# Routing stage of a graph and mixture-of-experts kernel: another way to the gate logits, and the sums formed on VectorE

## The reference

```python
# layer 1: messages along 25000 edges, sorted by their target row
H = layernorm(x).astype(f16);  v = edge_weight.astype(f16)
x = x + segment_sum(H[dst] * v[:, None], src)        # row to gather: dst, row to add to: src
# layer 2: a mixture of 8 experts, each token goes to one
h = layernorm(x)
logits = h @ gate_w + gate_b                          # (50000, 8)
probs = softmax(logits);  idx = argmax(probs);  prb = probs[idx]
pos = running count of idx, in token order            # place in the expert's queue
kept = pos < C                                        # C = ceil(1.25 * 50000 / 8)
y = relu(buf[e] @ w1[e] + b1[e]) @ w2[e] + b2[e]      # per expert, on its queue
x = x + nan_to_num(y * prb * kept)
```

## Time and profile before

| | us |
|---|---|
| median of three runs | 3391.64 |
| the profiled execution | 3385.78 |
| its span | 3384.2 |
| routing stage: first `slot_i` to last `slot_i` (48 steps) | 703.26 to 1252.62 |
| busy in the span: PE, DVE, ACT, POOL | 2856.8, 2205.4, 1627.8, 1881.3 |

### The profile page before, as it was taken

How to read it: one execution, slowest core, us unless ns; L and a number is a source line. 1 busy time by engine, 2 the same in 40 slices (tenths; PEclk the granted TensorE clock), 3 DMA queues, 4 the chain that set the end, 5 groups by cost and what they waited for, 6 DMA issues and landing times.

```text
span 3384.2 us, 63776 instructions
## 1 busy us (share of the span) xinstructions
PE 2856.8 (84%) x20366; PEld 2577.6 (76%) x20367; DVE 2205.4 (65%) x5550; ACT 1627.8 (48%) x2915; POOL 1881.3 (56%) x1680
## 2 busy tenths in 40 slices
PE   5733323289899976999999999999999999999998
PEld 4733223278788866989889898989899889898987
DVE  7934343377766644677766767777767676767766
ACT  3412121156655644555554555555555555555554
POOL 7788888756766765436354334536343454335333
PEclk8766666678867868999999999999999999999999
DMA  9644443386766623112112111212111121111111
GB/s 375 193 77 71 69 88 58 52 321 230 245 207 221 234 75 101 45 39 74 39 50 69 44 45 45 67 36 71 45 50 44 42 69 48 44 43 47 41 46 45
DMA packets 182245, 322.06 MB, mean 95 GB/s; under 512 B 97649, under 2 KB 124348, under 8 KB 166256
## 3 DMA queue, kind: packets, MB, share of 16 engines
q0 software_dynamic: 89696, 146.98, 16.7%
q1 hardware_dynamic: 92288, 172.66, 15.0%
q10 hardware_dynamic: 144, 1.05, 0.1%
HBM read 186.52 MB, written 138.79 MB: 96 GB/s over the span
## 4 chain that ended last, share of the span: by engine, by line
PE 57%; DVE 3%; issue 1%; DVEq 0%; POOL 0%; DMA 0%; SPq 0%; ACT 0%; POOLq 0%
PE u_Y L1353 29%; PE u_H L1339 26%; PE u_T L1321 2%; DVE y L1283 1%; DVE y L1278 1%; DVE yo L1297 1%; DVE yo L1294 0%; DVE low L1288 0%; DVE yo L1292 0%; DVE hlo L1265 0%; POOL u_x L1141 0%; DVEq L1264 0%; DMA u_x<-out_x,u_rec 0%; DVE u_token L1291 0%; DMA u_rec<-slots 0%
## 5 line engine op out<-in xcount | busy, mean ns | idle before, releaser
L1166 POOL DMA_INDIRECT out_x<-yo,u_token x348 | 435.8, 1252 | 761.0 <-DVE yo L1299 664.2
L1353 PE MATMUL u_Y<-whi,hhi 128*128 128x256 f32 x2784 | 788.2, 283 | 22.2 <-DVE hlo L1265 22.2
L1216 ACT ACTIVATE hm<-u_H,b1e 128x512 f32<-128x512 f32 (+1 forms) x736 | 489.0, 664 | 644.5 <-PE u_H L1339 618.9
L1353 PE MATMUL u_Y<-wlo,hhi 128*128 128x256 f32 x2784 | 779.7, 280 | 0.0
L1353 PE MATMUL u_Y<-whi,hlo 128*128 128x256 f32 x2784 | 779.4, 280 | 0.0
L1141 POOL DMA_INDIRECT u_x<-out_x,u_rec x380 | 396.5, 1043 | 363.4 <-issue 330.0
L1339 PE MATMUL u_H<-xhi,whi 128*128 128x512 f32 (+1 forms) x1472 | 571.5, 388 | 10.1 <-issue 10.1
L1339 PE MATMUL u_H<-xlo,whi 128*128 128x512 f32 (+1 forms) x1472 | 564.8, 384 | 0.0
L1339 PE MATMUL u_H<-xhi,wlo 128*128 128x512 f32 (+1 forms) x1472 | 564.5, 384 | 0.0
L1353 PEld LDWEIGHTS u_Y<-whi,hhi 128*128 128x128 f32 x2784 | 526.1, 189 | 25.3 <-DVE hlo L1265 25.3
L1353 PEld LDWEIGHTS u_Y<-wlo,hhi 128*128 128x128 f32 x2784 | 526.1, 189 | 0.0
(11 more groups left out here) (154 smaller groups left out, 4710.5 us busy)
## 6 DMA issues: line engine op xcount, KB each, us to landing
x<-in_x SPq DMA_DIRECT2D x49, 1024.0 KB
out_x<-x SPq DMA_DIRECT2D x49, 1024.0 KB, 5.0
agg<-zeros SPq DMA_DIRECT2D x25, 1024.0 KB
at<-agg SPq DMA_DIRECT2D x49, 512.0 KB, 5.8
raw<-in_L_ffn_w POOLq DMA_DIRECT2D x14, 1024.0 KB
src_row<-in_src SPq DMA_DIRECT2D x25, 512.0 KB, 4.8
slots<-rec,slot_i POOLq DMA_INDIRECT x392
u_x<-out_x,u_rec POOLq DMA_INDIRECT x380
```

Source lines behind the costliest of these rows:

```text
L1166: pool.indirect_dma_start(out=out[:, :], out_offset=bass.IndirectOffsetOnAxis(ap=token[:, s:s + 1], axis=0), in_=yo[:, s, :], in_offset=No ...
L1216: act.activation(hm[:, f, cols], ps_H[:, f % 2, cols], ACT.Relu, bias=b1e[:, f:f + 1])\
L1353: last = pe.matmul(ps_Y[:, s, 0:D], a[:, f, rows], w2_at(w, buf, f), start=(f == 0 and j == 0), stop=(f == KF - 1 and j == 2))
```

## The change

`aggregate`, its PSUM tile and the f16 identity go: VectorE adds the sums straight from `at` in SBUF. SyncE's load of `at` now waits for that addition. The four banks that this frees go to the turned rows, which now have four banks, and to the logits across (`ps_G`, 8 partitions by 1024 tokens).

`gate` now holds the gate weights (8 columns) and streams 256 turned tokens per product. ScalarE adds the bias as it copies `ps_G` to `across` (`add_bias`, two instructions of 8 by 512). `turn_back` transposes `across` back in eight small pieces, so that the tokens lie on partitions again and VectorE's `choice` reads the same `logits` tile as before. The bias product and `fill` go. The order on TensorE and ScalarE is written anew.

```diff
@@ SyncE, load @@
-                    sp.wait_ge(agg_up, s + 1 - AGGS)
+                    sp.wait_ge(x1_ready, s + 1 - AGGS)
@@ ScalarE @@
+            def add_bias(i, r):
+                s = RING * i + r
+                if not (isinstance(i, int) and s < 1):
+                    act.wait_ge(logits_ready, s)
+                for half in range(2):
+                    act.wait_ge(gated, BANKS * s + 2 * half + 2)
+                    part = slice(half * (STEP // 2), (half + 1) * (STEP // 2))
+                    act.activation(across[:, part], ps_G[:, part], ACT.Identity, bias=gb[:, 0:1])\
+                        .then_inc(across_ready, 1)
...
                 normalise(0)
                 normalise(1)
+                if not (isinstance(i, int) and s < 1):
+                    add_bias(*before_of(i, r, 1))
                 if not (isinstance(i, int) and s == LAST):
                     deviation(*next_of(i, r))
-                copy(0)
                 normalise(2)
-                copy(1)
                 normalise(3)
-                copy(2)
-                copy(3)
+                for k in range(BANKS):
+                    copy(k)
@@ TensorE @@
-            def aggregate(i, r):
...
-                for g in range(k * G // BANKS, (k + 1) * G // BANKS):
-                    for kd in range(KD):
-                        last = pe.matmul(logits[:, g, :], hT[:, g * KD + kd, :], gw[:, kd, :],
-                                         start=False, stop=(kd == KD - 1), skip_group_check=True)
-                if k == BANKS - 1:
-                    last.then_inc(gated, 1)
...
+                if not (isinstance(i, int) and s < 1) and k % 2 == 0:
+                    pe.wait_ge(across_ready, 2 * (s - 1) + k // 2 + 1)
+                part = hT[:, k * PER_BANK:(k + 1) * PER_BANK, :].rearrange("p (g kd) c -> p kd g c", kd=KD)
+                wide = STEP // BANKS
+                for kd in range(KD):
+                    last = pe.matmul(ps_G[:, k * wide:(k + 1) * wide], gw[:, kd, :], part[:, kd],
+                                     start=(kd == 0), stop=(kd == KD - 1))
+                last.then_inc(gated, 1)
+
+            def turn_back(i, r):
+                s = RING * i + r
+                pe.wait_ge(across_ready, 2 * (s + 1))
+                if not (isinstance(i, int) and s < 1):
+                    pe.wait_ge(hot_ready, s)
+                pe.nop(nofuse=True)
+                for g in range(G):
+                    last = pe.transpose(logits[:, g, :], across[:, g * P:(g + 1) * P], ident[0:E, 0:E])
+                last.then_inc(logits_ready, 1)
...
                 turn(i, r, 0)
                 turn(i, r, 1)
-                if isinstance(i, int) and s == 0:
-                    aggregate(0, 2)
-                else:
-                    rank(*before_of(i, r, 1))
-                    fill()
-                gate(i, r, 0)
-                turn(i, r, 2)
-                gate(i, r, 1)
-                turn(i, r, 3)
-                if not (isinstance(i, int) and s == 0):
-                    fill()
-                gate(i, r, 2)
-                if not (isinstance(i, int) and s > LAST - 3):
-                    aggregate(*((i, r + 3) if r + 3 < RING else (i + 1, r + 3 - RING)))
+                if not first:
+                    turn_back(*before_of(i, r, 1))
+                turn(i, r, 2)
+                turn(i, r, 3)
+                gate(i, r, 0)
+                gate(i, r, 1)
+                gate(i, r, 2)
+                if not first:
+                    rank(*before_of(i, r, 1))
                 gate(i, r, 3)
@@ VectorE @@
-                v.wait_ge(agg_up, s + 1)
+                v.wait_ge(agg_loaded[r % AGGS], 16 * ((RING // AGGS) * i + r // AGGS + 1))
                 v.wait_ge(x_loaded[r], 16 * (i + 1))
-                v.tensor_tensor(x1[:, r], ps_A[:], x1[:, r], ALU.add).then_inc(x1_ready, 1)
+                v.tensor_tensor(x1[:, r], at[:, r % AGGS], x1[:, r], ALU.add).then_inc(x1_ready, 1)
...
-                v.wait_ge(gated, s + 1)
+                v.wait_ge(logits_ready, s + 1)
```

More of the change, by code:

```diff
@@ L429, in route_tokens @@
     b1r = sb("b1r", [B1, P], F32)
-    gb = sb("gb", [P, E], F32)
-    ident16 = sb("ident16", [P, P], F16)
+    gb = sb("gb", [E, 1], F32)
+    across = sb("across", [E, STEP], F32)
     stats = sb("t_stats", [P, G, 6], F32)
@@ L454, in route_tokens @@
     ones, before, ident, eps = t["ones"], t["before"], t["ident"], t["eps"]
[L456 to L457 removed]
+    ps_T = ctx.enter_context(nc.psum_tensor("ps_T", [P, 4, 4, P], F32))
+    ps_G = ctx.enter_context(nc.psum_tensor("ps_G", [E, STEP], F32))
     ps_L = ctx.enter_context(nc.psum_tensor("ps_L", [P, 512], F32))
@@ L499, in route_tokens @@
     gated = sem("gated")
+    across_ready = sem("across_ready")
+    logits_ready = sem("logits_ready")
     hot_ready = sem("hot_ready")
@@ L510, in route_tokens @@
     BANKS = G * KD * P // 512
+    assert BANKS == 4
     PER_BANK = G * KD // BANKS
@@ L647, in copy @@
                 def copy(k):
-                    if k == 0 and not (isinstance(i, int) and s < 1):
-                        act.wait_ge(gated, s)
+                    if not (isinstance(i, int) and s < 1):
+                        act.wait_ge(gated, BANKS * (s - 1) + k + 1)
                     act.wait_ge(turned, BANKS * s + k + 1)
                     part = slice(k * PER_BANK, (k + 1) * PER_BANK)
-                    act.activation(hT[:, part, :], ps_T[:, k % 2], ACT.Copy).then_inc(hT_ready, 1)
+                    act.activation(hT[:, part, :], ps_T[:, k], ACT.Copy).then_inc(hT_ready, 1)
                 normalise(0)
                 normalise(1)
+                if not (isinstance(i, int) and s < 1):
+                    add_bias(*before_of(i, r, 1))
                 if not (isinstance(i, int) and s == LAST):
                     deviation(*next_of(i, r))
-                copy(0)
                 normalise(2)
-                copy(1)
                 normalise(3)
-                copy(2)
-                copy(3)
+                for k in range(BANKS):
+                    copy(k)
             deviation(0, 0)
+            act.wait_ge(consts, 48)
             steps(act, S, RING, body)
+            add_bias(S // RING, 0)
         @block.tensor
         def _(pe):
-            def aggregate(i, r):
-                s = RING * i + r
-                pe.wait_ge(agg_loaded[r % AGGS], 16 * ((RING // AGGS) * i + r // AGGS + 1))
-                if not (isinstance(i, int) and s == 0):
[L675 to L678, removed]
             def rank(i, r):
@@ L702, in gate @@
                 s = RING * i + r
-                q = r % 2
                 pe.wait_ge(hT_ready, BANKS * s + k + 1)
[L706 to L710, removed]
-                for g in range(k * G // BANKS, (k + 1) * G // BANKS):
-                    for kd in range(KD):
-                        last = pe.matmul(logits[:, g, :], hT[:, g * KD + kd, :], gw[:, kd, :],
-                                         start=False, stop=(kd == KD - 1), skip_group_check=True)
-                if k == BANKS - 1:
-                    last.then_inc(gated, 1)
[L718 to L722, removed]
+                if not (isinstance(i, int) and s < 1) and k % 2 == 0:
[9 more added lines that the diff above has]
+                pe.wait_ge(across_ready, 2 * (s + 1))
+                if not (isinstance(i, int) and s < 1):
+                    pe.wait_ge(hot_ready, s)
[3 more added lines that the diff above has]
+                last.then_inc(logits_ready, 1)
             def turn(i, r, k):
@@ L727, in turn @@
                 pe.wait_ge(h_ready, BANKS * s + k + 1)
-                if not (isinstance(i, int) and s < 1 and k < 2):
-                    pe.wait_ge(hT_ready, BANKS * s + k - 1)
+                if not (isinstance(i, int) and s < 1):
+                    pe.wait_ge(hT_ready, BANKS * (s - 1) + k + 1)
                 for n in range(PER_BANK):
                     g, kd = divmod(k * PER_BANK + n, KD)
-                    last = pe.transpose(ps_T[:, k % 2, n, :], h[:, q, g, kd * P:(kd + 1) * P], ident[:])
+                    last = pe.transpose(ps_T[:, k, n, :], h[:, q, g, kd * P:(kd + 1) * P], ident[:])
                 last.then_inc(turned, 1)
@@ L737, in body @@
                 s = RING * i + r
+                first = isinstance(i, int) and s == 0
                 turn(i, r, 0)
                 turn(i, r, 1)
-                if isinstance(i, int) and s == 0:
-                    aggregate(0, 2)
-                else:
-                    rank(*before_of(i, r, 1))
-                    fill()
-                gate(i, r, 0)
-                turn(i, r, 2)
-                gate(i, r, 1)
-                turn(i, r, 3)
-                if not (isinstance(i, int) and s == 0):
-                    fill()
-                gate(i, r, 2)
-                if not (isinstance(i, int) and s > LAST - 3):
-                    aggregate(*((i, r + 3) if r + 3 < RING else (i + 1, r + 3 - RING)))
```

(6 more changed lines are left out.)

6 lines of the change are left out of this document (1 added, 5 removed).

## The result

The changed kernel takes 3497.81 us (median of 6 runs, 3494.4 to 3502.26) against 3390.66 for the kernel before in the same sittings: a ratio of 1.033, 95% interval 1.030 to 1.036. It is slower by 107 us. The forecast was 3490, with 3440 to 3545 as its range.

The account below looks back on a forecast made before the run. It took the routing stage as bound by TensorE at low clock and GpSimd at high; after the change a loop gives 46 x 13.7 + 14 = 644 us plus 3, +98 against 549.4, so 3490 us, range 3440 to 3545.

Parts of the forecast that it names:

- the loop with a mixed clock: Routing stage: VectorE's pass plus the way through ScalarE and TensorE make one step, 13.7 us on average; 3490 us, chance 0.61.
- VectorE's pass, 8.47: Loop term: one pass of VectorE without a wait, from L831 to the end of L821, 8.47 us.
- To ScalarE and four normalisings: Loop terms after VectorE's pass: 0.12 us to ScalarE, then four normalisings there, 1.99 us.
- Bias and the way to TensorE: Loop term: two bias instructions on ScalarE, 1.00 us, and 0.22 to TensorE, 1.22 together.
- Small transposes: Last loop term: turn_back's eight transposes on TensorE, priced like old f32 gates, 1.01 us at full clock, 0.7 more at half.
- A gate instruction: TensorE, f32 product streaming 256 columns: 0.22 us at full clock, 0.44 at half, twice the nearest transpose.
- the rival at twice the price: Gates on TensorE: streaming f32 costs twice the value taken, a step about 15 us; 3553 us, chance 0.07.
- The rank: TensorE's rank, which VectorE needs at L861: 1.0 us late at half clock, in time at full clock.
- The clock: TensorE in the routing stage: low in the sparse part, high in the dense one, about half the time each.
- full clock, 3445: Rival, routing stage: TensorE's dense stretch keeps the clock at full, steps of 12.8 us; 3445 us, chance 0.12.
- The one that ended faster: Rival, routing stage: the loop does not bind and GpSimd's floor of 492 us does; 3335 us, chance 0.04.
- The collision of VectorE and GpSimd at the addition: Rival, VectorE's addition from SBUF: one scatter of 0.98 us per pass on top, +45 us; 3535 us, chance 0.04.

Follow-up runs that it names:

- after_fill: The changed kernel with twelve unread f16 products of 384 columns behind the last gate of each step: 3466.02 us, ratio 1.0196.
- both psum_sums runs: Changed kernel with sums through PSUM again: bias and turn_back ahead of the new step, 3358.48 us; or put back behind four normalisings and two turns, 3457.41 us.
- before_sbuf_sums: The kernel before with only the sums changed: VectorE adds them from SBUF, and TensorE's products with the identity go: 3484.94 us, ratio 1.0249.
- wide_gates_psum_sums: The changed kernel with sums through PSUM as before, bias and turn_back ahead of the new step, and gates and copies in the old order: 3358.48 us, ratio 0.9909.

## Why the prediction was right

The mechanism forecast as likeliest is the one that came: the loop with a mixed clock, a step of 13.7 us, of which 13.4 to 13.8 were measured, the stage 644 us of which 647.5 were measured, and 3490 against 3498. That the step is met to 0.1 us is in part luck, since two errors of about 0.5 us each, the small transposes and the rank below, cancel. The head was put at 3 us and is 6, and the 5 us behind the last slot_i weren't forecast. Point by point, by its own terms:

- VectorE's pass, 8.47: it is 9.24 in the step shown, and 0.66 of that is the wait for the rank. Without it, 8.58. The addition itself did not change (2.29).
- To ScalarE and four normalisings, 0.12 and 1.99: measured 0.12 and 1.98.
- Bias and the way to TensorE, 1.22: measured 1.23 + 0.14, 0.15 more. An instruction on 8 partitions and 512 values from PSUM took 0.66 us, not less than the 0.57 of the copy on 128 partitions.
- Small transposes, 1.01 at the full clock and 1.71 at half: over-priced. Eight took 0.63 us at the full clock and 0.99 at half, 0.81 in the step shown, where the clock falls among them. They start 62 ns apart at the full clock and 107 at half, where the old gates, with as many columns held and streamed, had 109 and 195 per instruction. "By the same type and form" was the weak step. Whether the transpose or the 8 rows in place of 128 makes the difference is not shown, so the reading of the Trainium skill put beside it, that 8 rows cost what 128 do, is not tested by this.
- A gate instruction, 0.22 and 0.44: measured 0.216 and 0.427 from start to start. Doubling the nearest row of the same type was right, and the rival at twice the price is out.
- The rank: at half clock 1.0 us late was forecast, in time at the full clock. Measured 44.9 us in 42 steps, 1.07 each, with the gates partly at each clock. It is the counterpart of the over-priced transposes: those were 0.4 to 0.7 too dear, while the rank is late in nearly every step, where the mean of the two loops counts it in half of them.
- The clock: half of the time at each level was expected, a mean of 0.75, and 0.75 it was; no row had given the half, so this is a guess that came true. The phase was wrong. The clock is not low in the sparse part and high in the dense one. It rises within the row of gates (the twelve of the step shown take 4.67 us, between the 2.6 of the full clock and 5.1 of half), stays high over the pause that follows, as the two turns there at 0.66 show, and in most steps falls during the small transposes. In the step shown TensorE was busy almost throughout before the clock rose (eight transposes and the gates), and idle for 2.9 us of the full-clock stretch before it fell.
- The rivals: full clock, 3445, is what after_fill gives in part: 3466 at 0.89. The one that ended faster needed the row outside VectorE's pass under 1.8 us; it is 4.3.
- The collision of VectorE and GpSimd at the addition, chance 0.04, is where the reasoning failed, though it did not cost here. It was argued down with L865, 0.05 us longer at worst. But the wrong partner was looked at: VectorE is not slowed, GpSimd is, by up to 2.1 us a scatter, and an operation of 0.23 us shows next to nothing of it: a scatter held until 0.85 us after such an operation gains 0.1 us at most. The Trainium skill's rule (SBUF — State Buffer, on which operations grab the shared pair), that a tensor_tensor with both inputs in SBUF contends with GpSimd's reads, is borne out by the trace with 3.08 against 0.98 us. The Trainium skill adds there that a probe did not show a tensor_tensor stalling DMA; here GpSimd's instruction for an indirect DMA is held. Which part of its work it is that waits, no run here shows.
- GpSimd's wait for slot_i was forecast at 160 us and is 121. The long scatters take 69 us of that time, and the first wait of the stage, 20.5 us, was not in the forecast.

## What to carry to other kernels

When an instruction of step s-1 is put behind one that waits for step s, follow the waits round once: if they come back to the same engine within one step, the whole way round is the length of a step, and each term in it counts once per step. A wait that shows in every step with the same length is the mark of such a loop. Before taking products off TensorE, count with its clock: here eight f16 products less in a step took it from 0.77 to 0.51 and cost 89 us. Before moving a sum from PSUM to SBUF inputs, look at what GpSimd does in that time, and cut the addition into pieces if it can't be avoided.

## What the runs showed of the hardware

- A VectorE tensor_tensor with two SBUF inputs of 2.29 us lengthens a GpSimd indirect DMA that starts just after it from 0.98 to 3.08 us. The DMA's instruction ends 0.85 us after VectorE's; one that already runs when the addition starts keeps its 0.98. In the changed kernel 45 of 392 scatters were over 1.2 us; in eight pieces of 0.35 us the longest was 1.33. With one input in PSUM (the kernel before and both psum_sums runs) none was over 1.06.
- At the full clock an f32 product that streams 256 columns starts 0.216 us after the one before, at half 0.427; a small transpose (8 rows and 128 columns held, 8 streamed) 62 and 107 ns.
- Busy time alone doesn't tell TensorE's clock: it was busy in 642 of 653 us at a granted clock of 0.51 in before_sbuf_sums, and in 423 of 511 us at 0.94 in wide_gates_psum_sums.
